# Two layers of attention and feed-forward: probabilities of the last six units of each layer scaled in place, output products of both heads in one sum

## What is computed

```python
x = x + attn0(layernorm(x))    # q, k normalised (RMS), rotated; window of 128
x = x + ffn0(layernorm(x))     # silu(gate) * up, 2 of 4 kept, down
x = x + attn1(layernorm(x))    # causal
x = x + ffn1(layernorm(x))     # silu(gate) * up, Hadamard transform, down

# attention, each batch and head:
probs = softmax(q @ k.T * scale + mask)
enc   = probs @ v
out   = sum over heads of enc[head] @ w_out[head]
```

## Time and profile before

| what | us |
|---|---|
| median of 3 runs | 708.91 |
| lowest, highest | 708.21, 710.39 |
| the profiled execution | 709.12 |
| its span, first to last instruction | 707.1 |

### The profile page before, as it was taken

One profiled execution on the slowest core, in us unless ns is written; L12 is line 12 of the kernel. 1 busy time (PEld: TensorE's weight loads), 2 busy tenths in 40 slices (PEclk: granted clock), 3 DMA queues, 4 the chain that ended last, 5 costly groups with the idle time before them and its releaser, 6 DMA issues.

```text
span 707.1 us, 16397 instructions
## 1 busy us (share of the span) xinstructions
PE 692.4 (98%) x4540; PEld 625.2 (88%) x4540; DVE 541.7 (77%) x1696; ACT 453.3 (64%) x1794; POOL 359.8 (51%) x557
## 2 busy tenths in 40 slices
PE   7999999999999998999999999999999999999998
PEld 3689999999999997888878999999999999987887
DVE  6879999999899988969845667766767777796443
ACT  4888888888888885423257666666666666664221
POOL 5998898898899844002069842323232323016100
PEclk9999999999999999999999999999999999999999
DMA  6010210101021010100021010101000100000000
GB/s 237 2 46 8 99 46 2 46 0 44 1 104 60 0 75 2 45 1 0 16 90 61 1 61 1 61 6 55 22 38 39 65 0 0 1 1 0 1 31 31
DMA packets 9033, 24.78 MB, mean 35 GB/s; under 512 B 912, under 2 KB 3088, under 8 KB 8848
## 3 DMA queue, kind: packets, MB, share of 16 engines
q1 hardware_dynamic: 8256, 22.55, 9.2%
q10 hardware_dynamic: 720, 1.57, 0.6%
HBM read 23.07 MB, written 1.05 MB: 34 GB/s over the span
## 4 chain that ended last, share of the span: by engine, by line
PE 86%; DVE 4%; issue 3%; POOL 3%; ACT 2%; DMA 1%; ACTq 0%; DVEq 0%; POOLq 0%
PE bank L508 12%; PE bank L885 11%; PE bank L398 11%; PE bank L500 10%; PE bank L527 7%; PE bank L366 5%; PE bank L412 5%; PE bank L430 5%; PE bank L359 4%; PE bank L435 3%; PE bank L959 3%; PE bank L450 3%; PE bank L963 2%; DVE x L658 1%; PE bank L979 1%
## 5 line engine op out<-in xcount | busy, mean ns | idle before, releaser
L658 DVE SCALAR_TENSOR_TENSOR x<-bank,rinv,x 128x256 f32<-128x256 f32 x256 | 123.1, 481 | 24.7 <-PE bank L398 22.5
L636 ACT ACTIVATE probs<-scores,negmax 128x128 f32<-128x128 f32 (+1 forms) x256 | 117.4, 471 | 9.7 <-DVE negmax L696 8.2
L544 ACT CAST turned<-bank 128x256 fp32r<-128x256 f32 x104 | 38.8, 373 | 102.5 <-PE bank L412 98.4
L774 POOL TENSOR_TENSOR a_hi<-raw_a,zero 128x384 fp32r<-128x384 f32 (+1 forms) x60 | 43.6, 726 | 84.6 <-PE bank L527 84.6
L669 DVE TENSOR_TENSOR enc_lo<-bank,enc_hi 128x256 fp32r<-128x256 f32 x128 | 54.2, 423 | 30.8 <-PE bank L366 21.1
L302 POOL TENSOR_TENSOR ln_r<-ln_ve,neg_half 128x1 f32<-128x1 f32 x26 | 17.0, 654 | 119.0 <-DVE ln_ve L276 118.9
L677 DVE TENSOR_TENSOR turned<-bank,turned 128x256 fp32r<-128x256 f32 x104 | 43.7, 420 | 40.5 <-ACT probs_t L545 40.5
L398 PE MATMUL bank<-b_hi,enc_hi 128*128 128x256 f32 x256 | 73.5, 287 | 0.0
L398 PE MATMUL bank<-b_hi,enc_lo 128*128 128x256 f32 x256 | 72.4, 283 | 0.0
L398 PE MATMUL bank<-b_lo,enc_hi 128*128 128x256 f32 x256 | 72.4, 283 | 0.0
L792 POOL TENSOR_TENSOR rot_a<-rot_a,rot_b 128x384 f32<-128x384 f32 x64 | 64.7, 1011 | 8.4 <-DVE rot_b L764 7.1
(11 more groups left out here) (179 smaller groups left out, 2397.8 us busy)
## 6 DMA issues: line engine op xcount, KB each, us to landing
raw_a<-in_wa SPq DMA_DIRECT2D x10, 768.0 KB, 4.4
raw_a<-in_wa SPq DMA_DIRECT2D x9, 512.0 KB, 4.0
raw_b<-in_wb SPq DMA_DIRECT2D x16, 256.0 KB, 2.6
hid_last<-in_wax SPq DMA_DIRECT2D x2, 512.0 KB, 4.9
w_a<-in_w2t SPq DMA_DIRECT2D x1, 1024.0 KB, 5.2
raw_b<-in_wdown SPq DMA_DIRECT2D x2, 512.0 KB, 3.1
x<-in_x SPq DMA_DIRECT2D x3, 256.0 KB, 5.7
raw_a<-in_wa ACTq DMA_DIRECT2D x1, 512.0 KB, 3.9
```

The source lines that it names most:

```text
L636: nc.scalar.activation(probs[:, c % 4, c0:c1], scores[:, c % 2, c0:c1], ACT.Exp, bias=negmax[:, c % 2, r:r + 1], scale=-1.0, accum_out=row ...
L658: nc.vector.scalar_tensor_tensor(out=x[:, m % 8, :], in0=output_bank(m)[:, hh * D:(hh + 1) * D], scalar=rinv[:, u, r:r + 1], in1=x[:, m % ...
```

## The change

For units 58 to 63 of each layer (`NORMAL_FROM = UNITS - 6`), the token tiles 2 to 7 of the last pair:

- `probs` is divided by its row sum before it is turned. In slot u+1 VectorE takes the reciprocal of unit u's two sums (semaphore `unitsum`), and ScalarE multiplies the blocks of 128x128 and 128x256 in place by it (semaphore `normal`). `pe_turn_probs` waits for `normal`.
- The output products of both heads then go as six passes into one sum in columns 0 to 255.
- `dve_residual` is one addition without `rinv` for these tiles.
- The pairwise `dve_rinv` of units 58 to 63 goes; the calls of `dve_rinv` move ahead of the second residual half.

```diff
                 for h in range(2):
+                    dst = output_bank(m)[:, 0:D] if both else output_bank(m)[:, h * D:(h + 1) * D]
                     for i, (l, r) in enumerate(PASSES):
-                        mm = pe.matmul(output_bank(m)[:, h * D:(h + 1) * D], enc[l][:, h, t * P:(t + 1) * P],
-                                       b_w[slot][r][:, h * D:(h + 1) * D], start=i == 0, stop=i == 2)
+                        mm = pe.matmul(dst, enc[l][:, h, t * P:(t + 1) * P], b_w[slot][r][:, h * D:(h + 1) * D],
+                                       start=i == 0 and not (both and h), stop=i == 2 and (h == 1 or not both))
...
                 need(pe, s["exp"], it, 2 * m + 2, 2)
+                if it is None and m >= NORMAL_FROM:
+                    pe.wait_ge(s["normal"], 2 * (m - NORMAL_FROM) + 2)
...
                 act_late_hi(act, c - UNITS + 2)
+            if it is None and NORMAL_FROM < c <= UNITS:
+                u = c - 1
+                act.wait_ge(s["unitsum"], u - NORMAL_FROM + 1)
+                for r, (c0, c1) in enumerate(((0, 128), (128, 384))):
+                    nc.scalar.mul(probs[:, u % 4, c0:c1], probs[:, u % 4, c0:c1], rinv[:, u % 16, r:r + 1]).then_inc(s["normal"], 1)
             if c >= TAIL_SLOT:
                 act_turned(act, L, it, c - 2)
...
-            if live(it, m) and m % 2 == 0:
+            if it is None and NORMAL_FROM < c <= UNITS:
+                u = c - 1
+                dve.wait_ge(s["exp"], 2 * u + 2)
+                nc.vector.reciprocal(rinv[:, u % 16, :], rowsum[:, u % 16, :]).then_inc(s["unitsum"], 1)
+            if live(it, m) and m % 2 == 0 and (it is not None or m < NORMAL_FROM):
...
-            if live(it, m):
+            if it is None and m >= NORMAL_FROM:
+                if hh == 0 and m < UNITS:
+                    dve.wait_ge(s["op"], m + 1)
+                    nc.vector.tensor_tensor(x[:, m % 8, :], output_bank(m)[:, 0:D], x[:, m % 8, :], ALU.add).then_inc(s["opadd"], 1)
+            elif live(it, m):
...
                     dve_heads_lo(dve, L, it, c)
+                    dve_rinv(dve, L, it, c)
                     dve_residual(dve, L, it, c, 1)
                     dve_scores_wait(dve, L, it, c)
                     dve_maxima(dve, L, it, c)
-                    dve_rinv(dve, L, it, c)
```

More of the change, by code:

```diff
@@ L54 @@
 SPLIT_SCORES = 8
+NORMAL_FROM = UNITS - 6
 FIRST_MEANS = LOOP_FROM + 3
@@ L226, in build @@
                  "proj", "vproj", "qkev", "vev", "sq", "ms", "rp", "rot", "radd", "roped", "tq", "tqev",
-                 "a0hi", "a0", "ahi", "a", "bhi", "b", "ptlo", "vlo", "qklo", "tqlo")
+                 "a0hi", "a0", "ahi", "a", "bhi", "b", "ptlo", "vlo", "normal", "unitsum", "qklo", "tqlo")
         at = [{n: sem(f"L{L}_{n}") for n in names} for L in range(2)]
@@ L395, in pe_output @@
                     need(pe, s["opadd"], it, m)
+                both = it is None and m >= NORMAL_FROM
                 for h in range(2):
+                    dst = output_bank(m)[:, 0:D] if both else output_bank(m)[:, h * D:(h + 1) * D]
                     for i, (l, r) in enumerate(PASSES):
-                        mm = pe.matmul(output_bank(m)[:, h * D:(h + 1) * D], enc[l][:, h, t * P:(t + 1) * P],
-                                       b_w[slot][r][:, h * D:(h + 1) * D], start=i == 0, stop=i == 2)
+                        mm = pe.matmul(dst, enc[l][:, h, t * P:(t + 1) * P], b_w[slot][r][:, h * D:(h + 1) * D],
+                                       start=i == 0 and not (both and h), stop=i == 2 and (h == 1 or not both))
                 mm.then_inc(s["op"], 1)
@@ L1174, in dve_drain0 @@
             dve_enc_lo(dve, 0, None, UNITS)
+            dve_rinv(dve, 0, None, UNITS)
             residual(1)
@@ L1177, in dve_drain0 @@
             stats(1)
-            dve_rinv(dve, 0, None, UNITS)
             for t in (2, 3):
@@ L1643, in tail @@
                         dve_enc_lo(dve, L, None, c)
+                        dve_rinv(dve, L, None, c)
                         dve_residual(dve, L, None, c, 1)
@@ L1651, in tail @@
                     ln_dve_ve(dve, st, t)
-                    if t == 1:
-                        dve_rinv(dve, L, None, c)
                 def head(c):
```

## The result

| | median, us | lowest to highest |
|---|---|---|
| before, measured beside it | 709.38 | 708.21 to 710.39 |
| with the change | 712.54 | 711.57 to 713.62 |
| forecast | 712.4 | 710.0 to 714.2 |

The ratio is 1.004, with a 95% interval of 1.0031 to 1.005: the change makes the kernel 3.2 us slower. The profiled execution took 712.54 us, its span 710.7.

A forecast was written before the change was run, and what follows sets the result against it. TensorE, busy 98%, bounds the kernel, so only its pauses count. Longer turns less drain savings give +1.6 us (layer 0) and +1.9 (layer 1): +3.5 on 709.12, 712.6; as median 712.4, range 710.0 to 714.2.

The forecast's parts named there:

- The price of a scaling: ScalarE's two in-place multiplications per unit take 0.71 us, like the two exponentials; bounds 0.53 and 0.89.
- B: Rival: the scaling is cheap, 0.53 us per unit as in the cast; +1.7, 710.6 us; chance 0.20.
- C: Rival: the scaling is dear, 0.89 us per unit without overlap; +5.3, 714.2 us; chance 0.09.
- The turn: Exponential to exponential in the last attention slots: 2.89 us, against 2.39 in layer 1 and 2.45 in layer 0.
- Rival A: The scaling hides in ScalarE's idle time and the drain gives what VectorE saves: -1.7, 707.2 us; chance 0.07.
- How many turns count: First scaling plus four turns, exponentials 60 to 63: `enc_hi` of unit 60 later by 2.5 (layer 0), 2.7 us (layer 1).
- What the drain gives back: Shorter residuals before the feed-forward: 0.39 and 0.44 us in layer 0, 0.3 and 0.5 in layer 1.
- later units gain nothing for TensorE: Layer 0 drain after `xn` of tile 2: TensorE next waits for `xT_lo`, which hangs on its own transposition.
- The first scaling: Slot 59, where ScalarE runs from one eviction to the next: the scaling costs its full 0.71 us.
- The sum: Layer 0 +1.6 and layer 1 +1.9 make +3.5 us: 712.6 on the profiled execution, 712.4 as median.
- The waits said to cost nothing: The transposition's wait for `normal`: scaling of unit u ends in slot u+1, TensorE wants it in slot u+2.
- the ring: ScalarE's exponential and `enc_hi`, VectorE's `enc_lo`, residual half and maximum, then the next exponential: 2.39 us in layer 1.

The follow-up runs named there:

- e3: Changed kernel plus a third ScalarE product of 128x256 per scaled unit, into memory nobody reads: 716.28 us, ratio 1.0098.
- e4: Changed kernel with ScalarE's scaling moved behind the `probs_t` copy, just before the next exponential: 709.06 us, ratio 0.9998.
- e5: Changed kernel with VectorE's reciprocal moved ahead of the low parts of the head's output (`enc_lo`): 708.4 us, ratio 0.9983.
- e12: e10 without the one sum: output products in two halves and two additions per unit, as before: 709.31 us against 709.80, ratio 0.9991.
- e10: Changed kernel with GpSimd scaling, after rotating the last heads; reciprocal between residual addition and `enc_lo`: 707.83 us against 709.19, ratio 0.9975.
- e1: Changed kernel without the scaling products and TensorE's wait for them; one sum and one addition stay: 708.37 us against 709.36, ratio 0.9987.

## Why the prediction held, point by point

**The price of a scaling, 0.71 us.** The two hold ScalarE for 0.71 us in every turn of layer 1. The neighbours chosen for it, the two exponentials, were the right ones, and rivals B (0.53) and C (0.89) are out. The estimate from the Trainium skill (ScalarE: Activation LUTs, "What ACT_TABLE_LOAD costs"), a fixed cost, a time per element and a surcharge for an operand read per partition, less an overlap, was 0.69, and the trace agrees with it to 0.02 us.

**The turn, 2.89 us.** Measured 2.87 in both layers (layer 0: exponentials at 264.05 and 266.92), term by term: 0.91 from `enc_hi` to the scaling against 0.39 + 0.33 + 0.20 = 0.92, 0.71, 0.36 against 0.37 to the exponential, and 0.89 to the next `enc_hi`. e3, e4 and e5 show that the place makes it: the same 24 instructions cost 4.1 us more behind a late reciprocal than behind an early one, and behind the early one nothing per turn but the first. Rival A (707.2) was right in its condition, that the reciprocal had to come before `enc_hi` ends: with it e5 reached 708.4. It fell short of A's time, 1.0 us below before instead of 1.7, since the first turn still cost 0.60 and 0.67, of which 0.46 and 0.67 were left at unit 63. The rule that the prediction weighed there, the Trainium skill's (Perfetto Trace Analysis, "Optimizing Scalar/DVE Operations") that work may go from a saturated VectorE to ScalarE, holds by e5 (708.4) and fails by the changed kernel (712.54), with the same instructions: it says nothing of the place, and the place decided.

**How many turns count.** Layer 1: forecast +2.7 at `enc_hi` of unit 60, measured +2.60. Layer 0: forecast +2.5, measured +1.98. This term was mis-sized. Four turns were taken at 0.44 each, but those of units 60 and 61 cost 0.25 and 0.28. The row that was overlooked lies in ScalarE's timeline of before, layer 0, the exponential of unit 61:

```profile
259.15 0.40 ACT L636 ACTIVATE probs<-scores,negmax 128x128 f32<-128x128 f32 x1 [1.02 <-DVE negmax L696]
```

The turns to units 60 and 61 were 3.45 and 3.24 us long, not 2.45, and had more idle time than the later ones' 0.5: ScalarE waited 1.02 for the maximum of unit 61, and 0.51 for that of unit 60 with 0.26 more ahead of `probs_t`. So more of the scaling hid, as I read it; no run tests these two turns alone. The first scaling cost 0.62 and 0.67, not 0.71.

**What the drain gives back.** Layer 0: the steps before `xn` of tiles 1 and 2 were forecast at 0.39 and 0.44. The offsets of the transpositions fall from +2.05 (270.06) to +1.67 (272.43) and +1.22 (274.58), by 0.38 and 0.45. Wrong was "later units gain nothing for TensorE": by the gate/up product the offset falls by another 0.38. Some 0.2 of that is the output product of unit 63, which in the kernel before starts at 278.15, right behind the two residual halves of unit 61 (277.00 to 278.00), and which with one addition does not wait. The other 0.15 lies between the transpositions of tiles 3 and 4; e12 has it too, without the sum, and its cause stays open. e12 against e10 gives the whole as 1.05. Layer 1: forecast 0.8, measured 2.61 - 1.79 = 0.82, and 0.75 by e12 against e10. Both terms were about right: forecast 0.3 by the first wide gate/up product and 0.5 behind it, measured 0.38 (that product starts at 639.66, before at 635.55, an offset of +2.23) and 0.44. That GpSimd's `ln_r` then binds is seen on VectorE of the changed kernel:

```profile
640.43 0.41 DVE L310 TENSOR_SCALAR xn<-x,ln_mv,ln_r 128x256 f32<-128x256 f32 x1 [0.34 <-POOL ln_r L303]
```

**The sum.** Forecast 1.6 + 1.9 = +3.5 us on the profiled execution; by the two drains it is 0.84 + 1.79 = +2.6, and the execution came out at 712.54 against 712.6 because its start, which the change does not touch, was 0.9 us slower. The medians say +3.2. So the mechanism and both layers' signs were right, layer 1 was right to 0.1 us, layer 0 was 0.8 too high (0.5 of turns and 0.3 of drain). The forecast also started from a median of 708.91, and the kernel before came to 709.38 when measured beside the changed one: a change of 3.5 us was forecast and 3.2 measured. That 712.4 came within 0.14 us of 712.54 is luck. What of the 0.5 us between +2.6 and +3.2 is spread between executions and what lies elsewhere stays open.

**The waits said to cost nothing.** TensorE's wait for `normal` appears nowhere as what ended a pause. One sign that the prediction named did not show: the value products do not wait longer for `enc_lo` (1.5 us in three waits before, 1.4 in six with the change). A part of TensorE's new idle time stands one product earlier, at the turning of probabilities, and is for `probs_t`, which the longer turn delays; in the list of waits of the changed kernel (total, times, longest):

```profile
PE bank L417 <- ACT probs_t L552: 2.4, 4, 0.8
```

What e10 shows is that even 0.97 us of scaling reaches TensorE in time if the turn is not longer. The reciprocals were put at 0.09 us per slot and off the path; e1 shows them at 0.06 per turn in the path as soon as the scaling no longer covers them.

## What to carry to other kernels

An engine's idle time can take new work only if the work stands where the idle time is: here ScalarE had 0.5 to 0.6 us idle in each turn, and 0.71 us of work cost 0.48 per turn behind a wait, 0.11 behind the same wait with `probs_t` moved into it, and nothing once its input came one instruction earlier. Before work is moved to another engine, write down one turn of the ring with the new instruction in its place, then ask which operand it waits for and which queue computes that; the cure is then often to move the producer, not the work. And take what stands at the end of a pipeline by the unit: the drain of layer 0 gained mostly by the units 58 and 59, layer 1 did as well with four units as with six. Last, a turn that comes out at the forecast length can still be set by another wait: add up the distances between starts, since a wait of 0.1 us has no bracket.
